# Patch embedding of an early-fusion transformer block: fp32 matmuls on the loaded image rows in place of three matmuls on rounded parts

## The reference, cut to what matters

```python
patches = X.reshape(B, C, N_PATCHES, PATCH, N_PATCHES, PATCH)      # B 64, C 3, N_PATCHES 8, PATCH 28
patches = patches.transpose(0, 2, 4, 1, 3, 5).reshape(B, N_PATCHES * N_PATCHES, IN_D)
tokens = jnp.einsum('bpi,hi->bph', patches, W) + b
...
return tokens * pos_embed[None, :, :]
```

## Time and profile before

| | before |
|---|---|
| median of 3 runs | 4013.82 us (4004.97 to 4017.44) |
| the profiled execution | 4009.25 us |
| its span in the profile | 4007.4 us |
| mean granted TensorE clock | 0.974 of full speed |
| first stage, from the start of the span to the first load of the second | 309.2 us |
| TensorE matmul busy in it | 191.9 us |
| ScalarE busy in it | 237.6 us |
| VectorE busy in it | 245.7 us |

### The profile page before, as it was taken

How to read it: one execution, slowest core, us unless ns; L and a number is a source line. 1 busy time by engine, 2 the same in 40 slices (tenths; PEclk the granted TensorE clock), 3 DMA queues, 4 the chain that set the end, 5 groups by cost and what they waited for, 6 DMA issues and landing times.

```text
span 4007.4 us, 72494 instructions
## 1 busy us (share of the span) xinstructions
PE 3529.6 (88%) x25120; PEld 2878.1 (72%) x25120; DVE 2588.1 (65%) x5052; ACT 1837.2 (46%) x2995; POOL 1557.5 (39%) x1318
## 2 busy tenths in 40 slices
PE   4776899999999999999899999999999999999998
PEld 4665677777777777777777777777777777777776
DVE  7885566666666666666656666666666666666664
ACT  6881244444444444444444444444444444434445
POOL 0001244433344444333444444334344443333445
PEclk9987899999999999999999999999999999999999
DMA  8760000000000000000000000000000000000000
GB/s 187 153 131 27 3 5 4 4 2 4 4 2 4 4 4 4 3 3 4 4 2 4 4 4 4 2 4 4 4 2 4 4 4 3 3 4 4 2 3 5
DMA packets 78353, 62.46 MB, mean 16 GB/s; under 512 B 6878, under 2 KB 76830, under 8 KB 77982
## 3 DMA queue, kind: packets, MB, share of 16 engines
q1 hardware_dynamic: 75906, 56.57, 6.6%
q10 hardware_dynamic: 2416, 5.48, 0.4%
HBM read 53.61 MB, written 8.42 MB: 15 GB/s over the span
## 4 chain that ended last, share of the span: by engine, by line
issue 53%; POOL 25%; PE 10%; DVE 3%; ACT 1%; POOLq 1%; ACTq 0%; DVEq 0%
POOL gelu L933 17%; POOL q_bd_hi L964 5%; PE bank L418 3%; POOL q_bd_lo L964 2%; PE bank L494 1%; PE bank L459 1%; PE bank L447 1%; POOL gst L946 1%; PE bank L453 1%; PE bank L427 1%; ACT gelu L866 1%; PE bank L431 1%; PE bank L428 1%; DVE gelu L628 0%; POOLq L932 0%
## 5 line engine op out<-in xcount | busy, mean ns | idle before, releaser
L933 POOL TENSOR_TENSOR gelu<-gelu 128x386 f32<-128x386 f32 x1024 | 1022.4, 1009 | 1856.1 <-ACT gelu L866 1853.3
L865 ACT ACTIVATE gelu<-bank,b_s 128x386 f32<-128x386 f32 x1024 | 595.8, 582 | 1458.2 <-DVE gelu L628 1453.4
L418 PE MATMUL bank<-gelu,w_s 128*128 128x386 f32 x2048 | 863.6, 506 | 104.3 <-POOL gelu L933 101.1
L628 DVE TENSOR_TENSOR gelu<-bank,ratio 128x386 f32<-128x386 f32 x1024 | 561.1, 553 | 372.0 <-PE bank L431 367.7
L866 ACT ACTIVATE gelu<-gelu,b_s 128x386 f32<-128x386 f32 x1024 | 624.7, 610 | 0.0
L427 PE MATMUL bank<-x_hi,w_hi 128*128 128x386 f32 x1024 | 493.4, 482 | 59.9 <-ACT gelu L865 58.1
L418 PEld LDWEIGHTS bank<-gelu,w_s 128*128 128x128 f32 x2048 | 367.5, 192 | 171.7 <-POOL gelu L933 156.1
L431 PE MATMUL bank<-x_lo,w_hi 128*128 128x386 f32 x1024 | 355.5, 347 | 8.9 <-DVE x_lo L811 8.9
L759 DVE TENSOR_TENSOR lp<-bank,con 128x512 f32<-128x512 f32 (+1 forms) x224 | 139.1, 633 | 336.4 <-PE bank L580 336.4
L742 DVE TENSOR_REDUCE mx<-bank 128x2 f32<-128x386 f32 (+1 forms) x416 | 226.0, 543 | 200.5 <-PE bank L536 200.4
L730 DVE TENSOR_TENSOR a_f<-bank,con 128x400 fp32r<-128x400 f32 x512 | 269.3, 565 | 130.2 <-PE bank L515 129.3
(11 more groups left out here) (167 smaller groups left out, 7610.9 us busy)
## 6 DMA issues: line engine op xcount, KB each, us to landing
xt<-in_x SPq DMA_DIRECT2D x192, 196.0 KB
txt_s<-in_txt SPq DMA_DIRECT2D x32, 128.0 KB, 2.1
out<-o_s SPq DMA_DIRECT2D x64, 48.5 KB
out<-o_s SPq DMA_DIRECT2D x64, 48.0 KB
rv<-in_rel_v ACTq DMA_DIRECT2D x1, 2624.0 KB, 16.8
w_s<-in_w ACTq DMA_DIRECT2D x1, 2048.0 KB, 16.1
tok_scratch<-tok SPq DMA_DIRECT2D x16, 128.0 KB, 5.0
tok<-tok_scratch SPq DMA_DIRECT2D x32, 64.0 KB, 1.9
```

What stands on the lines that cost most here:

```text
L418: mm(yb[:, 0:T2], w2_s[:, f, :], gelu1[:, f % RING, :], start=(f == 0), stop=(f == NF - 1)).then_inc(S["w2_done"], 1)
L628: v.tensor_tensor(gelu2[:, f % RING, :], zb[f % 2][:, 0:T2], ratio[:, :], ALU.mult).then_inc(S["z2_done"], 1)
L865: a(gelu1[:, f % RING, :], zb[f % 2][:, 0:T2], ACT.Gelu, bias=b1_s[:, f:f + 1]).then_inc(S["g_done"], 1)
L933: g.tensor_tensor(gelu1[:, f % RING, :], gelu1[:, f % RING, :], gelu2[:, f % RING, :], ALU.add).then_inc(S["hs_done"], 1)
```

## The change

The split into rounded parts goes. The weights lie in a tile of their own, `wt`, and TensorE multiplies them in fp32 with `xt` as it was loaded: for pixel s the moving operand is the 84x256 view with a step of 28 numbers. The zeroing of unused partitions, the copies to `xh`, the subtractions to `xl` and the split of the weights are gone, and with them all the work of VectorE and GpSimd in this stage (VectorE sets starting values of semaphores). `xt`, `tok` and the PSUM banks have four slots each (`SLOTS0`) in place of two. SyncE issues the weights and the loads of four batches without a wait, then loads batch i+4 when TensorE has done the last matmul of batch i (`x_used`). ScalarE copies the 256 tokens from PSUM and issues the store itself.

```diff
-PARTS0 = 4
+SLOTS0 = 4
...
-        wt_hi, wt_lo = sb("wt_hi", [P, PATCH, P], F32R), sb("wt_lo", [P, PATCH, P], F32R)
-        xt = sb("xt", [ROWS, 2, NB0 * NP_ * IMG])
-
-        xh, xl = sb("xh", [P, PATCH, n], F32R), sb("xl", [P, PATCH, n], F32R)
-        tok = sb("tok", [P, 2, n])
...
+        wt = sb("wt", [ROWS, PATCH, P])
+        xt = sb("xt", [ROWS, SLOTS0, n * PATCH])
+        tok = sb("tok", [P, SLOTS0, n])
+        ps = [ctx.enter_context(nc.psum_tensor(f"tok_ps{i}", [P, 512], F32)) for i in range(SLOTS0)]
...
         @block.sync
         def _(sp):
-            sp.dma_start(wt, a["w_tok"]).then_inc(w_in, 16)
-            load(sp, 0, 0)
-            sp.wait_ge(w_ready, 1)
-            load(sp, 1, 1)
-            with sp.Fori(0, NT0 // 2 - 1) as k:
-                for slot in range(2):
-
-                    sp.wait_ge(lo_ready, k * (2 * PARTS0) + (slot + 1) * PARTS0)
-                    load(sp, k * 2 + 2 + slot, slot)
-                    store(sp, k * 2 + slot, slot)
...
+            sp.dma_start(wt[:, :, :], a["w_tok"]).then_inc(w_in, 16)
+            for slot in range(SLOTS0):
+                load(sp, slot, slot)
+            with sp.Fori(0, NT0 // SLOTS0 - 1) as k:
+                for slot in range(SLOTS0):
+                    sp.wait_ge(x_used, k * SLOTS0 + slot + 1)
+                    load(sp, k * SLOTS0 + SLOTS0 + slot, slot)
...
         @block.tensor
         def _(pe):
...
-                    for q in range(PARTS0):
-                        pe.wait_ge(lo_ready, k * (2 * PARTS0) + slot * PARTS0 + q + 1)
-                        for s in range(q * QS, (q + 1) * QS):
-                            o = ps[slot][:, 0:n]
-                            mm(o, wt_hi[:, s, :], xh[:, s, :], start=(s == 0), stop=False)
-                            mm(o, wt_hi[:, s, :], xl[:, s, :], start=False, stop=False)
-                            m = mm(o, wt_lo[:, s, :], xh[:, s, :], start=False, stop=(s == PATCH - 1))
-                        m.then_inc(part_used, 1)
+            pe.wait_ge(w_in, 16)
+            with pe.Fori(0, NT0 // SLOTS0) as k:
+                for slot in range(SLOTS0):
+                    pe.wait_ge(tok_copied, k * SLOTS0 + slot + 1)
+                    pe.wait_ge(x_in[slot], k * (16 * C_IN * NB0) + 16 * C_IN * NB0)
+                    x = xt[:, slot, :].rearrange("p (n s) -> p s n", s=PATCH)
+                    for s in range(PATCH):
+                        m = nc.tensor.matmul(ps[slot][:, 0:n], wt[:, s, :], x[:, s, :], start=(s == 0), stop=(s == PATCH - 1))
+                    m.then_inc(x_used, 1)
...
         @block.scalar
...
+            with act.Fori(0, NT0 // SLOTS0) as k:
+                for slot in range(SLOTS0):
+                    act.wait_ge(x_used, k * SLOTS0 + slot + 1)
+                    act.wait_ge(tok_out[slot], k * 16 + 16)
+                    nc.scalar.activation(tok[:, slot, :], ps[slot][:, 0:n], ACT.Copy).then_inc(tok_copied, 1)
+                    act.wait_ge(tok_copied, k * SLOTS0 + slot + 1 + SLOTS0)
+                    act.dma_start(tok_scratch[:, bass.ds(k * (SLOTS0 * NB0) + slot * NB0, NB0), :],
+                                  tok[:, slot, :].rearrange("p (b n) -> p b n", b=NB0)).then_inc(tok_out[slot], 16)
```

More of the change, by code:

```diff
@@ L133, in patch_embed @@
         n = NB0 * NPATCH
-        wt_hi, wt_lo = sb("wt_hi", [P, PATCH, P], F32R), sb("wt_lo", [P, PATCH, P], F32R)
-        xt = sb("xt", [ROWS, 2, NB0 * NP_ * IMG])
-        xh, xl = sb("xh", [P, PATCH, n], F32R), sb("xl", [P, PATCH, n], F32R)
-        tok = sb("tok", [P, 2, n])
[L139 to L145, removed]
+        wt = sb("wt", [ROWS, PATCH, P])
+        xt = sb("xt", [ROWS, SLOTS0, n * PATCH])
+        tok = sb("tok", [P, SLOTS0, n])
+        ps = [ctx.enter_context(nc.psum_tensor(f"tok_ps{i}", [P, 512], F32)) for i in range(SLOTS0)]
+        w_in, x_used, tok_copied = sem("w_in"), sem("x_used"), sem("tok_copied")
+        x_in = [sem(f"x_in{i}") for i in range(SLOTS0)]
+        tok_out = [sem(f"tok_out{i}") for i in range(SLOTS0)]
         block = ctx.enter_context(nc.Block())
-        QS = PATCH // PARTS0
         def load(sp, i, slot):
@@ L154, in load @@
                     sp.dma_start(dst.rearrange("r (y w) -> r y w", w=IMG), src).then_inc(x_in[slot], 16)
[L156 to L163, removed]
         @block.sync
@@ L166, in _ @@
         def _(sp):
-            sp.dma_start(wt, a["w_tok"]).then_inc(w_in, 16)
-            load(sp, 0, 0)
-            sp.wait_ge(w_ready, 1)
-            load(sp, 1, 1)
-            with sp.Fori(0, NT0 // 2 - 1) as k:
-                for slot in range(2):
-                    sp.wait_ge(lo_ready, k * (2 * PARTS0) + (slot + 1) * PARTS0)
-                    load(sp, k * 2 + 2 + slot, slot)
-                    store(sp, k * 2 + slot, slot)
-            for slot in range(2):
-                store(sp, NT0 - 2 + slot, slot)
@@ L246, in _ @@
+            for slot in range(SLOTS0):
+                act.wait_ge(tok_out[slot], NT0 // SLOTS0 * 16 + 16)
         @block.vector
         def _(dve):
[L248 to L255, removed]
@@ L256, in _ @@
-            for slot in range(2):
-                dve.sem_inc(tok_out[slot], 16)
[L258 to L263, removed]
+            dve.sem_inc(tok_copied, SLOTS0)
@@ L265, in fused_block @@
+            for slot in range(SLOTS0):
+                dve.sem_inc(tok_out[slot], 16)
 def fused_block(nc, txt, w1, tok_scratch, out, R):
```

## The result

| | before | changed |
|---|---|---|
| median of 4 runs | 4009.39 us (4002.68 to 4017.44) | 4157.2 us (4150.22 to 4161.95) |
| the profiled execution | 4009.25 us | 4150.22 us |
| first stage, to the first load of the second | 309.2 us | 458.4 us |

The changed kernel is slower: ratio 1.0366, 95% interval 1.034 to 1.0393. The medians lie 147.8 us apart, and the forecast was 4157 us. The first stage alone grew by 149.2 us, against 147.6 forecast. In the pair of profiled executions the second stage, which is the same code, was 8.6 us shorter (3689.6 against 3698.2 us); that is within the scatter of the runs.

The account below looks back on a forecast made before the run. Rounding and remainder were taken to set the first stage's pace, loads close behind. Instead, 896 passes of 0.466 us (417.5 us) behind 36.7 us end at 454.2 against 306.6: 4009.25 + 147.6 = 4156.9, forecast 4157 us, range 4060 to 4220.

Parts of the forecast that it names:

- What bounds the kernel before: First stage: rounding and remainder set the pace, ScalarE's 64 roundings being 236 us of 270, with the loads close behind.
- The start at 36.7 us and the sum: First stage: TensorE starts once the first batch landed; 36.7 plus 417.5 us ends at 454.2 against 306.6, +147.6 us.
- The price of a pass, 0.466 us: First-stage matmuls: one of an fp32 matmul's two instructions, 256 stepped columns at ScalarE's 1.82 ns a number, 896 in all.
- I read that as a limit of the memory's side, ... not as one of either engine: Stepped reads of xt: ScalarE and VectorE share a memory limit, some 1.8 to 1.9 ns for each separate fetch.
- a TensorE that never idles should keep 1.00: First stage: clock goes from 0.92 of full speed to 1.00, which a pass waiting for memory doesn't feel.
- Rival 1: First-stage matmuls: the step costs TensorE nothing and loads set the pace; -63.3 us, 3946 us, chance 0.14.
- Rival 2: First-stage matmuls: TensorE's buffer half hides fetches, 0.30 to 0.42 us a pass; at 0.36 us +52.7 us, 4062 us, chance 0.06.
- Rival 3: First-stage fp32 matmuls: each number is fetched twice, 0.93 us a pass; +565 us, 4574 us, chance 0.06.
- Four slots bring nothing, loads hidden, stores hidden: First stage: TensorE's 26.1 us a batch covers a 12.95 us load and the token copy and store; two slots suffice.
- The 48 loads at the start: SyncE's load instructions for the first four batches: half a microsecond each, some 24 us, during which nobody waits for SyncE.

Follow-up runs that it names:

- E8: Changed kernel with ScalarE and VectorE packing each pixel's 256 numbers as neighbours, unrounded, fp32 matmuls on 128 partitions, two slots; 3960.23 us, ratio 0.9877 to the kernel before.
- E7: Kernel before with its three matmuls on 84 partitions in place of 128, same products; 4033.16 us, ratio 1.0064.
- E6: E5 with steps of 1, 4, 16 and 28 numbers in the four slots, wrong numbers in three; 4104.24 us.
- E4: Changed kernel with fp32r matmuls, step of 28, on a rounded copy made by ScalarE and VectorE, low parts left out, two slots; 3968.3 us, one run.
- E9: E4 on 128 partitions, each batch multiplied twice, slot 0 with the step of 28, slot 1 on neighbours; 3955.88 us.
- E11: Changed kernel with ScalarE also reading every batch with the step of 28 into a spare tile beside the matmuls; 4161.42 us, one run.
- E5: Changed kernel, step of 28 kept, on 128 partitions in place of 84, the 44 added ones zeros; 4160.46 us, ratio 1.0377 to the kernel before.
- E1: Changed kernel with each pixel's matmul reading 256 neighbouring numbers in place of numbers 28 apart, wrong products; 4122.49 us, ratio 1.0294 to the kernel before.
- E10: Changed kernel with two slots of xt, tok and PSUM in place of four; 4157.94 us, ratio 1.0371 to the kernel before.
- E2: Changed kernel with steps of 1, 2, 3 and 4 numbers in the four slots, wrong products; 4142.59 us, one run.
- E3: Changed kernel with steps of 5, 8, 16 and 28 numbers in the four slots, wrong products in the first three; 4169.54 us, one run.

## Why the prediction came out, point by point

- **What bounds the kernel before**: right as far as tried. A first stage without rounding and remainder runs at the pace of the loads (E8), and one whose TensorE is slowed to 0.213 us a pass is 25 us longer and bound by TensorE (E7).
- **The start at 36.7 us and the sum**: right. The stage grew by 1.6 us more than the sum: 0.1 us at the start, 1.0 in the passes, 0.5 in the tail. That the median met 4157 us to a microsecond is luck: the four runs lie between 4150 and 4162 us.
- **The price of a pass, 0.466 us**: right as a number (0.467 us), at both clocks. That single numbers 112 bytes apart bound it is shown by E6: 0.216 us without the step and 0.467 us with it, at full clock and with nothing else changed.
- **"I read that as a limit of the memory's side, ... not as one of either engine"**: the step that failed. ScalarE's 1.82 ns and TensorE's 1.82 ns a number are not one limit of a fetch. An fp32r pass takes 0.93 to 0.95 ns for each separate number (E4, E9), and ScalarE's reads and the matmuls don't disturb each other (E11). The forecast was right because fp32's price is twice that of fp32r and this double equals ScalarE's; whether the equality is chance no run shows, and the prediction had no ground for it. What it saw in ScalarE and VectorE stands: VectorE copies neighbours at 0.56 ns a number (E4, 2023 ns for 3584) and takes 1.93 ns with the step (E8, 3466 ns for 1792).
- **"a TensorE that never idles should keep 1.00"**: wrong. With 84 partitions it ran at 1.2 GHz from 36.8 to 454.6 us without an idle moment, and the 1.00 in the column there is not a measured clock. What saved the sum was the half sentence behind it, that a pass which waits for memory doesn't feel the clock: E5 has the full clock and the same time.
- **Rival 1 (3946 us if the step costs nothing)**: its price was wrong. With the step gone and the rest as it is the kernel takes 4122 us (E1), because of the clock. Two causes lay over each other, and either alone makes a pass of over 0.42 us: 0.427 us with the half clock and no step (E1), 0.467 us with the step and the full clock (E5). Taking away one of them gives 35 us (E1) or nothing (E5), taking away both gives the rival's time within 14 us (E8, 3960 us), of which some 11 us are, by the sum under E8, the token stores that it named.
- **Rival 2**: no such value turned up. **Rival 3**: the doubling for fp32 that it guessed is there (0.467 against 0.24 us), but from a base half as large as it took, since it put ScalarE's price on each sending. Its 4574 us was never near.
- **Four slots bring nothing, loads hidden, stores hidden**: right (E10; a DMA share of 0.46; SyncE waits 205.9 us for TensorE). The 48 loads at the start took longer to issue than I wrote (43 of them by 60.5 us, not 24 us for all), and nobody waited.

## What to carry to other kernels

Price a matmul by its moving operand's access pattern as well as by its columns: single fp32 numbers 16 bytes or more apart took 0.43 to 0.47 us a pass of 256 here against 0.216 us, so a copy that packs them is worth two engines' time when those engines are free, as in E8. Where a stage's matmuls use part of the partitions, read the durations of its weight loads before trusting the clock column, and try zero rows: 44 partitions of zeros brought the full clock in three comparisons here (the changed kernel and E5, E2 and E3 against E6, E7 and the kernel before). And when two causes each suffice, removing one shows little or nothing; an estimate that comes out exactly is no proof of its mechanism.

## What the runs showed of the hardware that I had not expected

- Matmuls on 84 partitions, fp32 or fp32r, kept TensorE at 1.2 GHz for a whole stage: 382.6 us without a gap in E1, 286.9 us in E7, 418 us in the changed kernel. With 128 partitions, the added ones all zeros, it came up to 2.4 GHz: at 44.2 us in E5, where the matmuls had begun at 39.8 us. The Trainium skill ("TensorE: Matmul & The Clock Gate", What's actually happening) has the clock follow how busy TensorE has been. Read as time without a pause, that rule would have a stage without a gap run at full clock, and these three did not. Whether the step between the two cases lies at 84 or elsewhere was not tried.
- The clock column reads 1.00 from the start of a program to the first change on record, whatever the clock is. In E7 the column says 1.00 over 287 us of passes at 0.213 us, and the first change on record, at 355.75 us, is a rise to full speed.
- A separate fetch costs TensorE the same at either clock: 0.467 us (fp32) and 0.24 us (fp32r) for 256 numbers. A step of 64 bytes is cheaper than 16, 20, 32 or 112 bytes (0.432 against 0.453 to 0.467 us).
